# A gram matrix from high and low fp32r parts of z, in two products and a sum with its own transpose

## What is computed

```
mod = (silu(c) @ wmod), cut into shifts, scales and gates (sa, ca, ga, sb, cb, gb), a row of each per batch
h   = layernorm(x) * (1 + ca) + sa
qkv = h @ w_qkv + b_qkv                                   # 8 heads of 64
scores = einsum('bhld,bhle->bhde', q, k) / 8              # 64 x 64 per head, summed over all 2048 tokens
out = einsum('bhld,bhde->bhle', v, softmax(scores)) @ w_fc + b_fc + h;  out = layernorm(out) * gamma + beta
x   = x + ga * out
h   = layernorm(x) * (1 + cb) + sb
x   = x + gb * sigmoid(xr @ W_r.T) * ((relu(xk @ W_k.T) ** 2) @ W_v.T)    # xr, xk: mixes of h with the token before
```

## Time and profile before

| what | us |
|---|---|
| median of 3 runs | 707.41 (706.69 to 708.01) |
| the profiled execution, its own time | 705.8 |
| its span, first to last instruction | 704.2 |
| one row of the loop | 82.05 |
| PE busy | 676.1 |
| DVE busy | 524.8 |
| ACT busy | 392.8 |
| POOL busy | 389.5 |

### The profile page before, as it was taken

How to read it: one execution, slowest core, us unless ns; L and a number is a source line. 1 busy time by engine, 2 the same in 40 slices (tenths; PEclk the granted TensorE clock), 3 DMA queues, 4 the chain that set the end, 5 groups by cost and what they waited for, 6 DMA issues and landing times.

```text
span 704.2 us, 11623 instructions
## 1 busy us (share of the span) xinstructions
PE 676.1 (96%) x3584; PEld 548.0 (78%) x3584; DVE 524.8 (75%) x1030; ACT 392.8 (56%) x871; POOL 389.5 (55%) x809
## 2 busy tenths in 40 slices
PE   7988999999999999999999999999999999998896
PEld 6767787978788887887879787888878878786665
DVE  4784898768878687868877688786878588467853
ACT  1434575556655475474755565554754747546552
POOL 5172885567275663586455672756635864326530
PEclk9999999999999999999999999999999999999999
DMA  9759255675846375573926657563755629616225
GB/s 317 220 166 210 90 158 91 130 163 113 194 86 146 120 158 118 97 177 89 217 77 133 162 117 184 89 151 111 165 116 92 124 57 199 117 29 153 30 31 89
DMA packets 90984, 93.02 MB, mean 132 GB/s; under 512 B 4224, under 2 KB 89000, under 8 KB 90960
## 3 DMA queue, kind: packets, MB, share of 16 engines
q0 software_dynamic: 33264, 33.03, 31.9%
q1 hardware_dynamic: 55344, 55.97, 24.9%
q10 hardware_dynamic: 2352, 3.73, 1.5%
HBM read 42.84 MB, written 33.10 MB: 108 GB/s over the span
## 4 chain that ended last, share of the span: by engine, by line
PE 34%; POOL 26%; issue 21%; DVE 9%; ACT 6%; DMA 2%; POOLq 1%; DVEq 0%; SPq 0%
PE work L1307 6%; PE att L1274 5%; PE gram L1256 5%; PE work L1324 4%; POOL x L483 4%; POOL ag L461 2%; ACT z L699 2%; POOL wv_aug L494 2%; PE tr L1249 2%; POOL ag_a L461 2%; DVE t_buf L894 2%; DVE mx L923 2%; POOL wv_aug L497 2%; PE gram L1385 2%; POOL rs_o L478 2%
## 5 line engine op out<-in xcount | busy, mean ns | idle before, releaser
L1274 PE MATMUL att<-m_sb,z_t 128*128 128x256 f32 x496 | 112.9, 381 | 8.4 <-DVE t_buf L894 7.6
L1274 PEld LDWEIGHTS att<-m_sb,z_t 128*128 128x128 f32 x496 | 92.4, 190 | 24.9 <-issue 13.7
L1324 PE MATMUL work<-mx,w_k_t 128*128 128x512 f32 x236 | 106.2, 592 | 0.0
L1307 PE MATMUL work<-w_r_t,mx 128*128 128x256 f32 x464 | 105.0, 379 | 0.0
L894 DVE SCALAR_TENSOR_TENSOR t_buf<-att,rs_o,g_row 128x256 f32<-128x256 f32 x124 | 51.4, 477 | 64.4 <-POOL rs_o L478 64.4
L1307 PEld LDWEIGHTS work<-w_r_t,mx 128*128 128x128 f32 x464 | 86.1, 190 | 10.4
L699 ACT ACTIVATE z<-x,ag 128x256 f32<-128x256 f32 x128 | 66.5, 598 | 48.6 <-POOL ag L471 48.6
L1256 PE MATMUL gram<-z 128*128 128x256 f32 (+1 forms) x512 | 89.7, 329 | 0.0
L449 POOL TENSOR_TENSOR ag<-st 128x4 f32<-128x4 f32 x32 | 18.6, 582 | 125.5 <-DVE st L905 125.5
L652 ACT ACTIVATE sq<-att 128x256 f32<-128x256 f32 x124 | 45.9, 382 | 72.4 <-PE att L1274 72.4
L1256 PEld LDWEIGHTS gram<-z 128*128 128x128 f32 x512 | 80.4, 192 | 6.7
(11 more groups left out here) (176 smaller groups left out, 1373.8 us busy)
## 6 DMA issues: line engine op xcount, KB each, us to landing
...
```

Source lines behind the costliest of these rows:

```text
L1274: ins = mm(att_banks(j, alone)[q][:, (t % 2) * D:(t % 2 + 1) * D], z_t[:, j, k, t * P:(t + 1) * P], m_sb[:, k], start=(k == 0), stop=(k == ...
L1307: ins = mm(r_banks(alone)[q][:, (t % 2) * D:(t % 2 + 1) * D], mixed(j, alone)[0][:, ch, tile], w_r_t[:, ch], start=(ch == 0), stop=(ch == ...
L1324: ins = mm(k_banks(alone)[dh][:], w_k_t[:, ch, rows_dh], mixed(j, alone)[1][:, ch], start=(ch == 0), stop=(ch == KD - 1))
```

## The change

z is stored doubled: POOL's factors are made with a quarter of the variance (constants 1/16 and a shrink of 0.25), and the column of ones becomes twos. ACT makes z_hi, which is half of that rounded to fp32r, in one instruction of 128x1024 per chunk. DVE makes z_lo = doubled z - 2 * z_hi, in one scalar_tensor_tensor of 128x1024 per chunk. z_hi has two buffers, z_lo one. PE adds z_hi'z_hi and z_lo'z_hi of each chunk into S, all as fp32r products of 256 columns: 16 for a chunk where there were four fp32 products of 256 columns and four of 128. After chunk 3 ACT copies half of S out in one instruction, PE transposes all four blocks, and DVE adds the two (`whole_gram`). The copies of the transposes get a scale of 0.5.

With the new steps the lists are written in another order at several places. In the row on DVE, `make_z(n, 3)` now comes ahead of `stats_2(b, 2)`, `low_z(n, 2)` ahead of `mix(b, 0)`, `low_z(n, 3)` behind `mix(b, 1)`, and `low_z(n + 1, 0)` ahead of `stats_a(n + 1, 3)` at the end of the row. On ACT `high_z` is put in five times. In the prologue `rows_b`, with what follows it, now comes behind `whole_gram(0)`, and `centre_fc` is cut in two.

```diff
             def high_z(b, j):                                     # ACT, new
+                act.wait_ge(z_ready, i + 1)
+                wait_past(act, z_used, i - 1)
+                nc.scalar.activation(z_hi[:, j % 2]..., z[:, j % 2]..., ACT.Copy, scale=0.5).then_inc(z_hi_ready, 1)
             def low_z(b, j):                                      # DVE, new
+                dve.wait_ge(z_ready, i + 1)
+                dve.wait_ge(z_hi_ready, i + 1)
+                wait_past(dve, z_used, i)
+                nc.vector.scalar_tensor_tensor(z_lo..., z_hi[:, j % 2]..., -2.0, z[:, j % 2]..., ALU.mult, ALU.add).then_inc(z_lo_ready, 1)
             def whole_gram(b):                                    # DVE, new
+                dve.wait_ge(gram_turned, b + 1)
+                nc.vector.tensor_tensor(g, g, gram[:], ALU.add).then_inc(g_ready, 1)
...
             def copy_gram(b):                                     # ACT
-                nc.scalar.activation(g_sb[:, 0], gram[:, 0:D], ACT.Copy)
-                nc.scalar.activation(g_sb[:, 1, P:D], gram[:, D:D + P], ACT.Copy).then_inc(g_up_ready, 1)
-            def copy_gram_low(b):
-                act.wait_ge(gram_turned, b + 1)
-                nc.scalar.activation(g_sb[:, 1, 0:P], gram[:, D + P:2 * D], ACT.Copy).then_inc(g_ready, 1)
+                nc.scalar.activation(g_sb..., gram[:], ACT.Copy, scale=0.5).then_inc(g_up_ready, 1)
...
             def turn_and_gram(b, j, first=False):                 # PE
-                for t in range(NT):
-                    for k in range(KD):
-                        ins = mm(gram[:, k * D:(k + 1) * D - k * P], z[:, j % 2, t, k * P:(k + 1) * P], z[:, j % 2, t, k * P:D],
+                pe.wait_ge(z_hi_ready, i + 1)
+                hi = z_hi[:, j % 2]
+                for n, rows_z in enumerate((hi, z_lo)):
+                    if n == 1:
+                        pe.wait_ge(z_lo_ready, i + 1)
+                    for t in range(NT):
+                        for k in range(KD):
+                            ins = mm(gram[:, k * D:(k + 1) * D], rows_z[:, t, k * P:(k + 1) * P], hi[:, t],
...
             def turn_gram(b):                                     # PE
-                nc.tensor.transpose(gram[:, D + P:2 * D], g_sb[:, 0, P:D], ident[:]).then_inc(gram_turned, 1)
+                for k in range(KD):
+                    for m in range(KD):
+                        ins = nc.tensor.transpose(gram[:, k * D + m * P:...], g_sb[:, m, k * P:(k + 1) * P], ident[:])
...
             def row_steps(b, first, far):                         # ACT: high_z(n, 2) ahead of copy_h2(b, 0),
                                                                   # high_z(n, 3) behind copy_h2(b, 1),
                                                                   # high_z(n + 1, 0), (n + 1, 1) around copy_h2(b, 3)
```

More of the change, by code:

```diff
@@ L87, in adaln_block @@
         last_c = sb("last_c", [P, D])
-        neg_half, half, quarter, minus_one, eps_att = (
-            sb(n, [P, NT]) for n in ("neg_half", "half", "quarter", "minus_one", "eps_att"))
+        neg_half, half, quarter, sixteenth, minus_one, eps_att = (
+            sb(n, [P, NT]) for n in ("neg_half", "half", "quarter", "sixteenth", "minus_one", "eps_att"))
         wqkv_sb = sb("wqkv_sb", [P, KD, 3 * HD])
@@ L133, in adaln_block @@
         z = sb("z", [P, 2, NT, D])
+        z_hi = part("z_hi", [P, 2, NT, D])
+        z_lo = part("z_lo", [P, NT, D])
         z_t = sb("z_t", [P, CH, KD, CT])
@@ L617, in copy_z_t, with high_z @@
                     act.wait_ge(z_turned, 2 * i + h + 1)
[L618 removed]
+                    nc.scalar.activation(z_t[:, j, h], tr[h][:], ACT.Copy, scale=0.5).then_inc(z_t_ready, 1)
             def copy_gram(b):
                 act.wait_ge(z_used, CH * (b + 1))
[L623 to L628 removed]
+                nc.scalar.activation(g_sb[:].rearrange("p k d -> p (k d)"), gram[:], ACT.Copy, scale=0.5).then_inc(g_up_ready, 1)
+            def high_z(b, j):
+                i = CH * b + j
+                act.wait_ge(z_ready, i + 1)
+                wait_past(act, z_used, i - 1)
+                nc.scalar.activation(z_hi[:, j % 2].rearrange("p t d -> p (t d)"), z[:, j % 2].rearrange("p t d -> p (t d)"),
+                                     ACT.Copy, scale=0.5).then_inc(z_hi_ready, 1)
             def copy_gq(b):
@@ L701, in make_z2, with row_steps @@
                 ins.then_inc(z2_ready, 1)
-            def row_steps(b, first):
+            def row_steps(b, first, far):
                 n = b + 1
@@ L783, in _ @@
             copy_pv(0)
-            row_steps(0, True)
-            with act.Fori(1, B - 1) as b:
-                row_steps(b, False)
+            high_z(1, 0)
+            high_z(1, 1)
+            row_steps(0, True, True)
+            with act.Fori(1, B - 2) as b:
+                row_steps(b, False, True)
+            row_steps(B - 2, False, False)
             last_row(B - 1)
@@ L886, in make_z, with low_z, whole_gram @@
                 ins.then_inc(z_ready, 1)
+            def low_z(b, j):
+                i = CH * b + j
+                dve.wait_ge(z_ready, i + 1)
+                dve.wait_ge(z_hi_ready, i + 1)
+                wait_past(dve, z_used, i)
+                nc.vector.scalar_tensor_tensor(z_lo[:].rearrange("p t d -> p (t d)"),
+                                               z_hi[:, j % 2].rearrange("p t d -> p (t d)").bitcast(F32), -2.0,
+                                               z[:, j % 2].rearrange("p t d -> p (t d)"), ALU.mult, ALU.add).then_inc(z_lo_ready, 1)
+            def whole_gram(b):
+                dve.wait_ge(gram_turned, b + 1)
+                g = g_sb[:].rearrange("p k d -> p (k d)")
+                nc.vector.tensor_tensor(g, g, gram[:], ALU.add).then_inc(g_ready, 1)
             def make_x2(b, j, mixes=None, alone=False):
@@ L1106, in _ @@
             stats_a(0, 3)
+            low_z(0, 1)
             make_z(0, 2, first=True)
@@ L1110, in _ @@
             make_z(0, 3, first=True)
+            low_z(0, 2)
             dve.wait_ge(wqkv_loaded, 16)
             prep_qk(0)
+            low_z(0, 3)
+            mean_fc()
+            whole_gram(0)
             rows_b()
```

52 lines of the change are left out of this document (37 added, 15 removed).

## The result

The changed kernel takes 744.89 us (median of 4 runs, 743.26 to 746.26) against 707.05 us (4 runs, 706.55 to 708.01): a ratio of 1.053, 95% interval 1.050 to 1.056. The span is 741.7 us against 704.2, and the mean granted clock of TensorE 0.970 against 0.991. The forecast was 743.7 us. It came so close partly because its errors cancel, as the end of this document shows.

The account below looks back on a forecast made before the run. A loop row was taken as bounded by a DVE and POOL chain, then PE back to back. Span 704.2 + 8.1 (prologue) + 5.7 (row 0) + 22.5 (six rows) = 740.5, median 743.7 us; range 719 to 755.

Parts of the forecast that it names:

- The frame: Loop row: DVE and POOL set make_m to t_buf(b, 1), so PE's saving there goes into waiting; z_lo lengthens that chain.
- stretch 1: Loop row from make_m to t_buf(b, 1), set by DVE and POOL: 30.27 us becomes 31.86.
- What PE sheds: Shorter gram products on PE save 0.74 us a chunk; with turn_gram's +0.33 a batch, 21 us in all.
- The hold of rstd_2(b, 0): POOL's last steps of rstd_2(b, 0) wait while DVE makes z_lo(n, 1): +0.4 us, open between 0 and 1.2.
- Stretch 2: Loop row from t_buf(b, 1) to ffn_r(b, 1): 27.34 us becomes 29.5, PE waiting 2.2 ahead of turn_z2(b, 2).
- X: Start of t_buf(b, 1) on DVE in a loop row, the zero from which the forecast counted times.
- O0 starts at 19.9: ffn_out(b, 0) on PE starts 19.9 us behind t_buf(b, 1), after DVE's low_k; PE could have had it at 19.3.
- The clock rival: PE's new pauses, chiefly ahead of turn_z2(b, 2), lower its clock: about 1.1 us more a row, prologue 2, 752 us; chance 0.15.
- Row 0: First row: z_hi(1, 2) delays copy_h2(0, 0) and z_lo holds POOL; ffn_r(0, 1) moves +5.7 us, 2.5 without holding.
- copy_h2(0, 0) mechanism: First row: z_hi(1, 2) on ACT moves copy_h2(0, 0) from 73.63 to 78.2; transposes of (1, 2) and mix(0, 0) wait.
- Prologue: Before the rows: z_hi and z_lo work delays rows_b and POOL's factors, so wv_attn(0) moves +8.1 us (7 to 10).
- The sum: Whole kernel: 704.2 + 8.1 + 5.7 + 22.5 = 740.5 us of span, median 743.7.

Follow-up runs that it names:

- e8: Changed kernel with the old f32 gram products on z in place of the two fp32r ones, all other new steps kept: 750.9 us, ratio 1.061.
- e3: Changed kernel without any z_lo, the second product taking z_hi on both sides: 723.6 us, ratio 1.024.
- e5: Changed kernel with, in rows 1 to 6, POOL's rstd_o(b,1) ahead of prep_wv(n) and ACT's squares(b,1) ahead of make_z2(b,0): 734.9 us, ratio 1.040.
- e1: Changed kernel with low_z(n + 1, 0) behind stats_a(n + 1, 3) at the end of the row on DVE: 743.3 us, ratio 1.052.
- e4: Changed kernel with 17 more transposes filling PE's wait between turn_z2(b,0) and attention(b,2) in rows 1 to 6: 761.9 us, ratio 1.079.
- e10: Changed kernel with z_hi(1,2) behind copy_h2(0,0) on ACT, in row 0 alone: 744.3 us, ratio 1.052.

## Why the prediction was right, point by point

- **The frame held.** Most of PE's saving (1.75 of 2.7 us a row, e8) is idle because the chain over DVE and POOL ends stretch 1 (e3, e8, e5), and z_lo is most of the loss of the loop (e3).
- **What PE sheds** was put at 0.74 us a chunk and is 0.63: from product to next work the gram takes 1.99, not 1.88. (With the transposes ahead of it, which make way 0.08 sooner, it is 0.71.) It changed nothing.
- **Stretch 1**: z_lo ahead of stats_a was put at +1.19 and is +1.13. The hold of rstd_2(b, 0) was put at +0.4, two small steps; it is +1.0, since z_lo meets the power instruction at its very start (337.04 and 337.05). Forecast +1.6, measured +2.15.
- **Stretch 2**: t_buf(b, 2) at X + 12.98 is at X + 13.30. The forecast 29.5 (rstd_2(b, 2) 6.3 us, PE's wait 2.2) is what happens at full clock: 29.87, 6.5 and 2.18 in e1's fast row. In the kernel after it is 28.44, 4.0 and no wait, since attention(b, 2) ran slow. The step that failed is "O0 starts at 19.9", with all of PE's work ahead of it at full clock: it starts at 20.8 (366.39), for attention(b, 2) took 5.38 us. That this came out 1.1 us shorter, and not longer, is luck.
- **The clock rival** had a chance of 0.15, and its mechanism came, at another pause (ahead of attention(b, 2), 2.08 us) than the one it named. Its price, +1.1 a row, was wrong in sign there: it took the place of the other wait. At the pause that it did name it costs 1.7 a row (e4, e5), but only in kernels in which attention(b, 2) runs fast. The forecast had itself named PE's wait of over 2 us ahead of attention(b, 2), and did not ask what it does to the clock.
- **Row 0**: +5.7 was +7.8. ffn_r(0, 1) starts 6.5 later against make_m(0), and then takes 4.94 us in place of 3.62 behind the wait of 2.28 us ahead of turn_z2(0, 2). The copy_h2(0, 0) mechanism is seen (PE waits 2.27 us) but is worth 0.2 (e10).
- **Prologue**: +8.1 was +10.7. The DVE chain was right to 0.8 us (whole_gram at 41.2 for 41.0 at its end, rows_b at 41.80). Behind it POOL's first V weights took 3.14 us for 2.35 and the factors 0.4 more. wv_attn(0) started at 58.41, not 56.6, and took 3.55 for 2.74, at a granted clock of 0.54. The main forecast had no slow clock in the prologue. Timelines of POOL and PE, beside the earlier trace rows:

```profile
46.83 3.14 POOL L499 TENSOR_TENSOR wv_aug<-wv_t,rows 128x1024 f32<-128x1024 f32 x1 [19.43 <-issue]
```

```profile
58.41 3.55 PE L1434 MATMUL att<-wv_aug,attn 128*128 128x256 f32 x8 [3.58 <-POOL wv_aug L509]
```

- **The sum**: prologue 2.6 and row 0 2.1 too low, the loop 3.2 and the last row 0.3 too high. Net 1.2. The total was better than its terms, and that is luck. So may be the 1.6 us that the forecast put between the profiled execution and the median: it is again 1.6, but two of the four executions are near 743.5 us and two near 746.2. A slow make_m(0), as in e1 and e10, would be worth 2 us of that, but no trace shows the longer two.
